# Attention on TensorE: products into a shared PSUM bank issued whole at a unit's end, maxima turned later

## The reference

```python
q = einsum('oc,bct->bot', Wq, target) + bq      # the same for k and v from the source
q = q.reshape(b, 16, 16, t)                     # 16 heads of 16 channels; k, v alike
dot = einsum('bhdt,bhds->bhts', q, k) / sqrt(16)
dot = mask * dot - (1 - mask) * 1e6
amap = softmax(dot, axis=-1) * mask
out = einsum('bhts,bhds->bhdt', amap, v)
x = layernorm(x + out)                          # before the feed-forward block
```

## Time and profile before

| | us |
|---|---|
| median of three timed runs | 3245.24 |
| lowest, highest | 3241.58, 3249.78 |
| the profiled execution | 3250.03 |
| its span in the trace | 3248.2 |
| TensorE busy | 2971.8 (91%) |
| VectorE busy | 2824.2 (87%) |
| ScalarE busy | 2360.5 (73%) |
| GpSimd busy | 1990.9 (61%) |

### The profile page before, as it was taken

The page is one execution under the profiler, slowest core; times in us unless marked ns, Lnnn a source line. Parts: engine busy times, 40 slices in busy tenths (PEclk is TensorE's granted clock), DMA queues, the critical chain, the costliest instruction groups (busy, mean ns, idle before and its releaser), DMA issues. The chain is left out here.

```text
span 3248.2 us, 47812 instructions
## 1 busy us (share of the span) xinstructions
PE 2971.8 (91%) x16101; PEld 1814.1 (56%) x16134; DVE 2824.2 (87%) x4149; ACT 2360.5 (73%) x4499; POOL 1990.9 (61%) x1071
## 2 busy tenths in 40 slices
PE   8899999999999999999976998888889888789998
PEld 5677777776777767776653433333333333244444
DVE  6999999999999999999995788888788888188886
ACT  5888888888888888888871366666666666567876
POOL 4999999999999999999993132232223222100000
PEclk9999999999999999999986699999999999899999
DMA  4202220122202220122224455555555553131111
GB/s 172 68 9 78 82 79 28 61 79 79 73 18 78 82 79 32 58 79 79 86 78 115 126 164 168 179 173 161 173 163 169 167 179 92 65 109 46 43 43 36
DMA packets 138148, 312.49 MB, mean 96 GB/s; under 512 B 20240, under 2 KB 27536, under 8 KB 137760
## 3 DMA queue, kind: packets, MB, share of 16 engines
q1 hardware_dynamic: 132544, 300.05, 29.3%
q10 hardware_dynamic: 5360, 9.38, 1.0%
HBM read 217.42 MB, written 91.95 MB: 95 GB/s over the span
## 5 line engine op out<-in xcount | busy, mean ns | idle before, releaser
L823 POOL TENSOR_TENSOR bu<-du,bc 128x1024 f32<-128x1024 f32 x512 | 1199.4, 2372 | 32.3 <-DMA bc<-bc_scratch 32.0
L710 ACT ACTIVATE states<-dt,negA 128x256 f32<-128x256 f32 x2048 | 852.6, 463 | 239.5 <-DVE hc L918 229.0
L1560 DVE TENSOR_REDUCE mmax<-s_ps 128x1 f32<-128x512 f32 x1024 | 671.7, 685 | 202.8 <-PE s_ps L1292 185.5
L906 DVE TENSOR_TENSOR_SCAN states<-states,bu 128x512 f32<-128x512 f32 x704 | 821.4, 1212 | 9.0 <-ACT states L710 8.1
L1416 ACT ACTIVATE pt<-s_ps 128x512 f32<-128x512 f32 x1024 | 549.0, 595 | 342.6 <-PE s_ps L1302 341.7
L918 DVE TENSOR_TENSOR hc<-states,bc 128x512 f32<-128x512 f32 x704 | 445.2, 673 | 1.2 <-DMA bc<-bc_scratch 1.2
L1292 PE MATMUL s_ps<-kst,qst 51*128 51x512 f32 x1024 | 400.0, 470 | 40.8 <-DMA kst<-mask_d 21.4
L528 PEld LDWEIGHTS y_ps<-id_sb,hc 128*128 128x128 f32 x2816 | 331.1, 143 | 122.4 <-DVE hc L918 58.0
L528 PE MATMUL y_ps<-id_sb,hc 128*128 128x128 f32 x2816 | 377.1, 277 | 23.4 <-DVE hc L918 23.4
L1302 PE MATMUL s_ps<-qst,kst 53*128 53x512 f32 x1024 | 385.5, 455 | 4.3 <-ACT pt L1416 4.3
L832 POOL TENSOR_TENSOR hp<-hp,bc 128x1024 f32<-128x1024 f32 x160 | 379.7, 2373 | 1.6 <-DVE hp L906 1.1
(11 more groups left out here) (164 smaller groups left out, 4218.8 us busy)
## 6 DMA issues: line engine op xcount, KB each, us to landing
bc<-bc_scratch SPq DMA_DIRECT2D x128, 512.0 KB, 5.0
stack_d<-parts SPq DMA_DIRECT2D x90, 512.0 KB, 3.8
qst<-stack_d SPq DMA_DIRECT2D x128, 192.0 KB
kst<-stack_d SPq DMA_DIRECT2D x128, 192.0 KB
x<-xres SPq DMA_DIRECT2D x31, 512.0 KB, 4.4
w_raw<-in_w_ffn SPq DMA_DIRECT2D x48, 256.0 KB, 2.7
w_raw<-in_w_ffn SPq DMA_DIRECT2D x16, 768.0 KB, 7.2
xT_sb<-in_xT SPq DMA_DIRECT2D x16, 512.0 KB, 5.9
```

Source lines behind the costliest of these rows:

```text
L710: a = act.activation(states[:, bank, first:first + SEQ], dt[:, t, :], ACT.Exp, scale=negA[:, t, c * NS + n:c * NS + n + 1])
L823: pool.tensor_tensor(bu[:, buf, :].rearrange("p (n l) -> p n l", n=NS), du[:, t % (2 * GRP):t % (2 * GRP) + 1, :].to_broadcast([P, NS, SEQ ...
L906: dve.tensor_tensor_scan(dst, src, bu[:, BU_OF[k][0], cols], 0.0, ALU.mult, ALU.add).then_inc(scan_done, 1)
L1560: dve.tensor_reduce(mmax[:, u // HG, c:c + 1], s1_ps[:, n % S_BANKS], AX.X, ALU.max).then_inc(s1_free, 1)
```

## The change

`shared` loses its two parts: it issues the whole product, and is called once in a unit, behind pair 3. So all of it, the wait for the bank's reader and the waits for inputs too, stands behind the last pair. On ScalarE the copies of turned maxima move from the end of the unit in which they are turned to the next unit, behind its first two exponentials, and `mask_values` moves from the unit's end to the same place. VectorE, GpSimd and SyncE have the same order as before.

```diff
-            def shared(pos, b, par, part):
+            def shared(pos, b, par):
...
-                if part == 0:
-                    before = misc_before(pos, b)
-                    if before is not None:
-                        pe.wait_ge(ev[before[0]], before[1])
+                before = misc_before(pos, b)
+                if before is not None:
+                    pe.wait_ge(ev[before[0]], before[1])
...
-                cuts = [0, len(products) // 2, len(products)]
-                for dst, lhsT, rhs, start, stop in products[cuts[part]:cuts[part + 1]]:
...
-                if products and part == 1:
-                    m.then_inc(mm[kind], 1)
+                m.then_inc(mm[kind], 1)
...
                         if tt == 1 and g < 0 and active(n):
                             values(n, 1 - par, HGROUPS - 1, u % HG)
-                        if tt == 1 or tt == 3:
-                            shared_part(u, tt // 2)
+                    for pos, (unit, kind, _, off) in enumerate(MISC):
+                        if unit == u and has(kind, b + off):
+                            shared(pos, b, par)
...
-                    for kind, unit in SPLIT_AT.items():
-                        if u == unit and active(f):
-                            round_part(kind, f)
-                    if u % HG == HG - 1:
-                        g, batch = (u // HG - 1, b) if u >= HG else (HGROUPS - 1, n)
-                        if active(batch):
-                            copy_values(batch, g)
-                    if active(b):
-                        exponentials(b, u, 1)
                     for unit, kind, idx, off in MISC:
-                        if unit == u and kind == "m" and active(b + off):
+                        if unit == u - 1 and kind == "m" and active(b + off):
                             act.wait_ge(mm["m"], seq("m", b + off, idx))
...
                     for unit, kind, idx, off in MISC:
                         if unit == u - 1 and kind == "v" and active(b + off):
                             mask_values(b + off, 1 - par, idx)
+                    for kind, unit in SPLIT_AT.items():
+                        if u == unit and active(f):
+                            round_part(kind, f)
+                    if u % HG == HG - 1:
...
+                    if active(b):
+                        exponentials(b, u, 1)
```

More of the change, by code:

```diff
@@ L1316, in values @@
                     m.then_inc(pv_done, 1)
[L1318 removed]
+            def shared(pos, b, par):
                 _, kind, idx, off = MISC[pos]
                 batch = b + off
[L1322 to L1334 removed]
+                before = misc_before(pos, b)
+                if before is not None:
+                    pe.wait_ge(ev[before[0]], before[1])
+                else:
+                    pe.wait_ge(kq_params, 3 * 16)
+                if isinstance(b, int) and b == -1 and kind in "mv":
+                    pe.wait_ge(params, 4 * 16)
+                    pe.wait_ge(vaug_set, 1)
                 if kind in "kq":
[L1337 removed]
+                    if kind == "k" and isinstance(batch, int) and batch == 1:
                         pe.wait_ge(ctx1_in, 16)
[L1339 removed]
+                    elif kind == "k":
                         pe.wait_ge(ctx_in, batch * 16)
[L1341 removed]
+                    if kind == "q":
                         pe.wait_ge(ln_done, batch)
@@ L1346, in shared @@
                             cols = slice(a * (HID // 2), (a + 1) * (HID // 2))
-                            product(misc[:, cols], w[:, k, idx * P:(idx + 1) * P], src[:, k, cols], k == 0, k == SEQT - 1)
+                            m = pe.matmul(misc[:, cols], w[:, k, idx * P:(idx + 1) * P], src[:, k, cols],
+                                          start=(k == 0), stop=(k == SEQT - 1))
                 elif kind == "v":
-                    if part == 0 and isinstance(batch, int) and batch == 0:
+                    if isinstance(batch, int) and batch == 0:
                         pe.wait_ge(ctx_in, 16)
@@ L1353, in shared @@
                         for k in range(SEQT):
-                            product(misc[:, a * SEQ:(a + 1) * SEQ], ctx_sb[:, 1 - par, k, st * P:(st + 1) * P],
-                                    wv_sb[:, k, :], k == 0, k == SEQT - 1)
+                            m = pe.matmul(misc[:, a * SEQ:(a + 1) * SEQ], ctx_sb[:, 1 - par, k, st * P:(st + 1) * P],
+                                          wv_sb[:, k, :], start=(k == 0), stop=(k == SEQT - 1))
                 elif kind == "turn":
-                    if part == 0:
-                        pe.wait_ge(o_copied, (batch + 1) * HGROUPS)
+                    pe.wait_ge(o_copied, (batch + 1) * HGROUPS)
                     for g in range(HGROUPS):
-                        product(misc[:, g * P:(g + 1) * P], o_sb[:, (batch * HGROUPS + g) % OSB, idx * P:(idx + 1) * P], id2[:, :])
+                        m = pe.transpose(misc[:, g * P:(g + 1) * P], o_sb[:, (batch * HGROUPS + g) % OSB, idx * P:(idx + 1) * P], id2[:, :])
                 elif kind == "back":
-                    if part == 0:
-                        pe.wait_ge(ev["turn"], (batch + 1) * TT)
+                    pe.wait_ge(ev["turn"], (batch + 1) * TT)
                     for tt in range(TT):
-                        product(misc[:, tt * P:(tt + 1) * P],
-                                on_sb[:, tt, idx * 8:(idx + 1) * 8, :].rearrange("p h d -> p (h d)"), id2[:, :])
-                elif part == 0:
+                        m = pe.transpose(misc[:, tt * P:(tt + 1) * P],
+                                         on_sb[:, tt, idx * 8:(idx + 1) * 8, :].rearrange("p h d -> p (h d)"), id2[:, :])
+                else:
                     pe.wait_ge(s1_free, score(batch, (MAXIMA[idx][-1] + 1) * HG, 0))
@@ L1371, in shared @@
                         m = pe.transpose(misc[0:HG * TT, i * P:(i + 1) * P], mmax[:, g, :], id2[:, :])
-                    m.then_inc(mm["m"], 1)
-                cuts = [0, len(products) // 2, len(products)]
-                for dst, lhsT, rhs, start, stop in products[cuts[part]:cuts[part + 1]]:
-                    if kind in ("turn", "back"):
-                        m = pe.transpose(dst, lhsT, rhs)
-                    else:
-                        m = pe.matmul(dst, lhsT, rhs, start=start, stop=stop)
-                if products and part == 1:
-                    m.then_inc(mm[kind], 1)
+                m.then_inc(mm[kind], 1)
             def body(b, par):
                 s, n = b + 1, b - 1
-                def shared_part(u, part):
-                    for pos, (unit, _, _, off) in enumerate(MISC):
-                        if unit == u and has(MISC[pos][1], b + off):
-                            shared(pos, b, par, part)
                 for u in range(HEADS):
@@ L1483, in body @@
                             mask_values(b + off, 1 - par, idx)
+                    for kind, unit in SPLIT_AT.items():
+                        if u == unit and active(f):
+                            round_part(kind, f)
+                    if u % HG == HG - 1:
+                        g, batch = (u // HG - 1, b) if u >= HG else (HGROUPS - 1, n)
+                        if active(batch):
+                            copy_values(batch, g)
+                    if active(b):
+                        exponentials(b, u, 1)
                     if u == 14 and active(f + 1):
```

11 lines of the change are left out of this document (removed).

## The result

The changed kernel takes 3156.53 us, median of four runs (3153.21 to 3179.05); the kernel before took 3245.5 beside it (3241.58 to 3249.78). The ratio is 0.974, with a 95% interval of 0.9693 to 0.9787. The forecast was 3168.0, in a range of 3145 to 3205: right in sign and mechanism and 11 us too long.

The account below looks back on a forecast made before the run. Bound: a chain between TensorE and VectorE through the shared bank. Thirteen passes at 5.25 us less (63.56 to 58.31) plus 9.5 elsewhere give 78 off 3250.0, 3172; timed median 4.8 lower, 3168, range 3145 to 3205.

Parts of the forecast that it names:

- Hidden wait at the new place: Behind pair 3 the product may begin at 1.94 us into the unit; TensorE arrives at 2.31, so the wait is hidden.
- Whole product, 2.06: TensorE's joined product: two halves cost 2.12 us, less about 0.06 for one seam, so 2.06.
- Units bound by VectorE, 3.30: Turning units, set by VectorE's own work with TensorE keeping up, go from 3.74 to 3.30 us.
- Rival 1: VectorE's units (5 to 10, 13 to 15) gain nothing, about 2.3 us per pass remains: 3210 us; chance 0.12.
- Unit 1: Whole k product follows pair 3, which waits for VectorE's row behind norm statistics: 3.77 us against 2.77, losing 1.0.
- Maxima later and ScalarE's order: 0: Turned maxima copied later, and ScalarE's copies standing between its two halves of exponentials, cost 0.
- Rival 2: ScalarE's copies delay exponentials, about 1 us in five units of each pass: 3240 to 3250 us; chance 0.04.
- Opening pass and pass 0, 3 and 2: Estimated gains: 3 us in the opening pass, at half clock, and 2 us in pass 0, which has no turning.
- rivals (5): More than forecast: opening-pass clock rises to 2.4 GHz earlier, up to 18 us more; chance 0.09 for under 3150.
- Pass 14 and what follows, 3.5 + 1: Estimated gains: 3.5 us in pass 14, without k or q product, and 1 us in pass 15, without maxima.
- Rival 3: TensorE's clock falls to 1.2 GHz, adding 48 us a pass; with two such passes 3265 us; chance 0.03.
- Rival 4: Maxima rows land late, each us beyond the slack costing 13 us; slower only from 6 us beyond, chance 0.02.

Follow-up runs that it names:

- the experiment with the early place: Kernel before with the whole product behind pair 1 and the values, and ScalarE's changed order: 3323.2 us, ratio 1.0222.
- Moving the statistics: Changed kernel with the next unit's norm statistics moved from the end of unit 0 to units 11 and 12 of the pass before: 3133.01 us.
- ScalarE's part alone: Kernel before with only ScalarE's loop of the changed kernel; TensorE keeps its halves: 3257.4 us, ratio 1.0013.
- change again: The changed kernel, unedited, run once more beside the kernel before: 3155.16 us, ratio 0.9704.
- interleaved: Kernel with moved norm statistics, its products reordered so VectorE-heavy and TensorE-heavy units alternate, statistics in units 10 and 12: 3166.49 us, ratio 0.9718.
- only turns, back, maxima late: Kernel before with ScalarE's changed order and only turned outputs, turned back and maxima whole behind pair 3; k, q, v in halves: 3213.05 us.
- opening pass alone: Kernel before with whole late products in the opening pass only, later passes in halves: 3238.16 us, ratio 0.9974.
- TensorE's part alone: Changed kernel with ScalarE's loop put back to its order of before; products whole behind pair 3: 3153.99 us, ratio 0.9699.
- only k, q and v whole: Kernel before with ScalarE's changed order and only k, q, v products whole behind pair 3, the rest in halves: 3205.53 us, ratio 0.9857.

## Why the forecast came out as it did

*The bound.* Right: a chain between TensorE and VectorE over the shared bank, at the place the prediction named. Waits of the products are all but gone, and the experiment with the early place shows the chain by making it longer.

*Hidden wait at the new place.* Right: 0.7 us left in 610.

*Whole product, 2.06.* Mis-sized: 1.92. The term that failed is the seam, estimated at 0.06 from 1.13 of rows with a 1.06 step; it is 2 x 1.06 - 1.92 = 0.20. So a unit bound by TensorE is 4.25, not 4.37 (2.31 + 1.92 = 4.23). Five units show it: 1, 3, 4, 11 and 12 are 3.64, 3.97, 4.25, 4.12 and 4.24, against 3.77, 4.2, 4.37, 4.2 and 4.37, together 0.7 less; unit 2, set by VectorE, is 4.64 against 4.66. With it the working's 58.31 becomes 57.6, and 57.55 was measured. "They can't cost more" was right, the size of the seam wrong by a factor of three.

*"Inside that 89% TensorE waits."* Misread: the waits are the other 11%. From 1890 to 2500 us TensorE was shown idle for 65.9 of 610 us, 6.9 a pass, and the groups above with 1.3 us of another make up all of it. Of the 6.0 gained a pass, 4.8 came out of that idle time and 1.2 out of busy time, the seams.

*Units bound by VectorE, 3.30.* Right to the hundredth: 3.30. Rival 1 (they gain nothing) is dead: alone, they bring 3.5 a pass.

*Unit 1.* Right: row 0 to row 0 takes 2230.40 - 2226.76 = 3.64, forecast 3.77, the rest being the seam. Moving the statistics gave 1.39 a pass, 1.75 in unit 0 less 0.28 in unit 1 and 0.1 in unit 12.

*Maxima later and ScalarE's order: 0.* Right in the changed kernel (57.55 against 57.54 without it), while the same order costs 0.47 a pass in the kernel before. The step that the working left out is that these copies free the bank: with `back` behind pair 1 TensorE waits 0.40 for them, with `back` behind pair 3 they are done. Rival 2, delayed exponentials, was not seen.

*Opening pass and pass 0, 3 and 2.* The opening is mis-sized: 9.35. The step that failed is costing it at a fixed half clock. Pass 0 is right: 2.03. The rise of the clock stood among the rivals (5), with 0.09, and it came, without carrying the total below 3150.

*Pass 14 and what follows, 3.5 + 1.* Measured 10.7, and for another reason. Last score after pass 14's first row, and the granted clock between:

| kernel, profiled | last score after row 0 of pass 14 | of it at low clock |
|---|---|---|
| before | 102.1 | from about 2803 on, 12 us |
| ScalarE's part alone | 97.7 | none |
| change | 91.7 | none |
| change again | 91.7 | none |
| interleaved | 114.5 | from about 2682 on, 54 us |
| only turns, back, maxima late | 114.5 | from about 2732 on, 53 us |
| opening pass alone | 122.2 | from about 2769 on, 61 us |

Before, and then the last kernel of the table, with TensorE at work nearly all of the time:

```profile
2805.00:2815.00 10.00, 9.74 (x35) 2.76 (x28) 0.69 (x1) 4.25 (x8) 0.00 (x0) 0.50 0.34 88
```

```profile
2745.00:2765.00 20.00, 18.12 (x104) 7.45 (x102) 13.62 (x22) 13.65 (x29) 5.37 (x2) 1.00 0.08 29
2770.00:2830.00 60.00, 58.18 (x180) 17.23 (x178) 4.34 (x10) 29.35 (x55) 11.26 (x5) 0.50 0.13 40
```

From unit 15's first row to the last score, products in halves take 45.9 us at full clock (ScalarE's part alone); with the low clock it is 70.8 in the last kernel of the table and 50.7 before, so each us at the low clock adds 24.9 / 61 = 0.41, or 4.8 / 12 = 0.40. In the changed kernel it is 44.7. So pass 14 up to its unit 15 gave 4.4 (51.4 to 47.0; forecast 3.5), fewer waits behind it 1.2 (45.9 to 44.7; forecast 1), and 4.8 is clock: the execution of before lost it there and the one of after did not. That is a property of the executions as much as of the kernels. It agrees with the medians being only 89 apart where the profiled executions are 97 apart, and a loss of 20 to 25 us there would account for runs such as 3179 of the changed kernel or 3265 of the last experiment, and, in three of four of its runs, for the interleaved kernel (3137.34 beside 3162.93, 3170.04 and 3172.18). The mean granted clock of those runs agrees: 0.976 in the first of these four and 0.963 to 0.966 in the others, 0.967 at 3179.05 and 0.970 to 0.974 in the other runs of the change. Only profiled executions show the place; for the others it is inferred. Why the clock falls there in one execution and holds in another stays open.

*Rival 3, the clock falls: slower.* It fell once in the steady stage of the profiled execution, and for a few us, not for a pass. TensorE in unit 1 of that pass, then at the end of the low stretch:

```profile
2285.36 0.50 PE L1292 MATMUL s_ps<-kst,qst 51*128 51x512 f32 x1 [1.52 <-DVE mmax L1541]
...
2285.80 2.78 PE L1341 MATMUL misc<-ctx_sb,wk_sb 128*128 128x256 f32 x8
2288.51 0.79 PE L1292 MATMUL s_ps<-kst,qst 51*128 51x512 f32 x1
...
2289.66 1.34 PE L1313 MATMUL pv_ps<-pt,vaug 128*32 128x512 f32 x8
2290.93 0.50 PE L1292 MATMUL s_ps<-kst,qst 51*128 51x512 f32 x1
```

Pair 3 waited 1.52 for VectorE's row behind the statistics (1.21 in the pass shown above, where the clock stayed), and the product behind it takes 2.78 in place of 1.99. That pass took 59.29 in place of 57.54. The Trainium skill, "TensorE: Matmul & The Clock Gate", section on psum-queue depth-cycling, describes frequent small idles between groups of matmuls that make the clock swing between its two levels. Here the trace agrees only in part. Against my reading in the prediction it was the change that put an idle of over 1 us in front of a product, where the kernel before had none; but the clock fell behind one such idle of twelve (1890 to 2640 us), and did so again at the same place in the change run again (1.54) and in TensorE's part alone (1.53). With only k, q and v whole, the same idle cost no clock, and the product behind it takes 2.00:

```profile
2312.58 0.49 PE L1293 MATMUL s_ps<-kst,qst 51*128 51x512 f32 x1 [1.52 <-DVE mmax L1565]
```

With the product whole at the early place, idles of 1.05 and 1.46 stand in every pass and the clock fell in two of them; in the interleaved kernel it fell once, behind an idle of 0.89, while the kernel before had idles up to 0.96 and no fall. So the length of the idle alone does not decide it. With the statistics moved the wait is gone and the clock stays at 1.00 from 1890 to 2640 us.

*Rival 4, maxima rows land late.* Not seen: scores for ScalarE, which wait for them, idle 0.0 us from 1890 to 2500 us; with the shortest pass (statistics moved) it is 0.5, of which 0.4 for those rows.

By stretch, the errors against the profiled executions are + 6.35 (opening), 0.0 (pass 0), + 8.1 (passes 1 to 13: 0.76 a pass, less the 1.75 of the pass with the low clock) and + 6.2 (end, 4.8 of it clock), none of them the other way, 20.6 together and less the later start 19; as the medians differ by 8 us less than the profiled executions, 11 of it is left in the result. They don't cancel; the range was wide enough for their sum. The seam is 9 us of them and the clock, which the sum held at nothing, up to 11: 4.8 at the end and most of the opening's 6.35.

## What to carry to other kernels

Where two engines share one bank, draw the loop through it, with every instruction that stands between the product and its evacuation on the reading engine: put the product so that the reading engine's queue reaches the evacuation while the writing engine still has other work, and only then join the halves. The place was worth 4.1 us a pass here and the joining 1.9, while joining at the wrong place cost 4.6 to 5. The same holds for every reader of the bank: ScalarE's later copies cost 0.47 until the product behind them moved too. What stands ahead of the first row after such a move (here, norm statistics) is late next; moving them was worth another 22 us.

## What the runs showed of the hardware

A group of eight f32 products of 128x256 costs 1.92 us in one piece and 2 x 1.06 in two: 0.20 for one break, three times my estimate. A pair of scores alone between halves costs 0.44, two pairs 0.66. A unit that VectorE sets costs the same 3.30 at every turn, with no idle.

The clock is less steady than one profile shows. In the opening pass it was 0.50 from 1770 to 1790 us before and 0.79 after, depending on where products stand; in the closing stage it fell in some executions and stayed low for up to 61 us, with TensorE shown busy for 58.18 of 60 us; and in one pass of the changed kernel it fell behind a wait of 1.52 us, at the same place (2280 to 2290 us) when the change was run again, while the same wait in another kernel cost nothing. The second of these is the costly one, up to 25 us of one execution, and no experiment here says what sets it off.
